# Window attention: V as the stationary operand in four column groups, fp32 probabilities streamed whole, and the bias carried through the projection

## What is computed

```python
x = x + attention(group_norm(x))        # x: 8 x 56 x 88 x 192, fp32
# group_norm: 32 groups of 6 channels, mean and variance over a whole image
# attention, on windows of 7 x 11 = 77 tokens, 8 heads of 24:
qkv  = xw @ qkv_w + qkv_b
attn = softmax(q @ k.T / sqrt(24))      # 77 x 77 for each head and window
out  = (attn @ v) merged over heads     # 77 x 192
out  = out @ proj_w + proj_b
```

## Time and profile before

| | us |
|---|---|
| median of 3 runs | 2111.34 (2107.02 to 2124.22) |
| the profiled execution, its own time | 2107.97 |
| its span, first to last instruction | 2105.9 |
| PE busy in the span | 1691.6 (80%) |
| POOL busy | 1608.9 (76%) |
| DVE busy | 1515.2 (72%) |
| ACT busy | 1299.1 (62%) |
| first and last `neg_max` of the 256 slots start at | 209.4 and 2066.0 |

### The profile page before, as it was taken

One profiled execution on the slowest core, in us unless ns is written; L12 is line 12 of the kernel. 1 busy time (PEld: TensorE's weight loads), 2 busy tenths in 40 slices (PEclk: granted clock), 3 DMA queues, 4 the chain that ended last, 5 costly groups with the idle time before them and its releaser, 6 DMA issues.

```text
span 2105.9 us, 97027 instructions
## 1 busy us (share of the span) xinstructions
PE 1691.6 (80%) x41742; PEld 1500.7 (71%) x41742; DVE 1515.2 (72%) x3672; ACT 1299.1 (62%) x2659; POOL 1608.9 (76%) x2060
## 2 busy tenths in 40 slices
PE   0003899988898888988898989988898889988886
PEld 0002788877787778877787878777787778887775
DVE  6772677777677776777777777777777777777783
ACT  0002667767676676766676766766676666767763
POOL 0004689888888898888888998988888888988864
PEclk9999899999999998999999998999999999999996
DMA  6881101111111111111111111111111111111110
GB/s 159 226 232 39 45 20 51 46 57 40 38 57 57 56 57 57 42 54 40 41 54 57 57 57 57 57 39 57 39 50 46 57 57 57 57 48 48 39 39 38
DMA packets 17134, 127.74 MB, mean 61 GB/s; under 512 B 1921, under 2 KB 2178, under 8 KB 2434
## 3 DMA queue, kind: packets, MB, share of 16 engines
q1 hardware_dynamic: 16770, 121.91, 17.1%
HBM read 91.62 MB, written 30.28 MB: 58 GB/s over the span
## 4 chain that ended last, share of the span: by engine, by line
PE 58%; DVE 26%; issue 10%; DMA 3%; ACT 1%; POOL 1%; DVEq 1%; SPq 0%; ACTq 0%; POOLq 0%
PE ps_a L676 25%; PE ps_q L676 8%; PE ps_q L775 6%; PE ps_k L676 6%; PE ps_s L715 6%; DVE v_lo L587 5%; DVE v_hi L641 5%; DVE q_lo L588 5%; DMA x_stat<-in_x 3%; PE ps_b L761 3%; DVE y_blk L627 2%; PE ps_b L676 2%; DVE q_hi L634 2%; DVE k_lo L588 2%; DVE stat L541 2%
## 5 line engine op out<-in xcount | busy, mean ns | idle before, releaser
L343 POOL TENSOR_TENSOR p_lo<-probs,p_hi 77x1232 f16<-77x1232 f32 x256 | 646.8, 2526 | 220.2 <-ACT p_hi L404 217.0
L434 ACT ACTIVATE probs<-ps_s,exp_shift,exp_scale 77x1232 f32<-77x1232 f32 x256 | 351.8, 1374 | 258.1 <-PE ps_s L715 246.1
L676 PE MATMUL ps_a<-v_hi,p_hi 77*128 77x25 f16 x4096 | 362.8, 174 | 84.6 <-DVE v_lo L587 81.9
L676 PEld LDWEIGHTS ps_a<-v_hi,p_hi 77*128 77x128 f16 x4096 | 330.1, 97 | 124.4 <-issue 122.0
L588 DVE SCALAR_TENSOR_TENSOR q_lo<-ps_q,b_qk,q_hi 128x154 f16<-128x154 f32 x512 | 170.4, 376 | 327.9 <-PE ps_q L775 327.9
L596 DVE TENSOR_REDUCE neg_max<-ps_s 77x16 fp32r<-77x1232 f32 x256 | 365.8, 1429 | 34.5 <-PE ps_s L730 34.5
L676 PE MATMUL ps_a<-v_hi,p_lo 77*128 77x25 f16 x4096 | 361.6, 174 | 0.0
L676 PE MATMUL ps_a<-v_lo,p_hi 77*128 77x25 f16 x4096 | 361.2, 174 | 0.0
L676 PEld LDWEIGHTS ps_a<-v_lo,p_hi 77*128 77x128 f16 x4096 | 323.3, 97 | 0.0
L676 PEld LDWEIGHTS ps_a<-v_hi,p_lo 77*128 77x128 f16 x4096 | 321.8, 97 | 0.0
L404 ACT ACTIVATE p_hi<-probs 77x1232 f16<-77x1232 f32 x256 | 310.0, 1211 | 0.3
(11 more groups left out here) (147 smaller groups left out, 5693.5 us busy)
## 6 DMA issues: line engine op xcount, KB each, us to landing
x_stat<-in_x SPq DMA_DIRECT2D x16, 1848.0 KB, 9.9
x_norm<-in_x SPq DMA_DIRECT2D x32, 924.0 KB
y_blk<-in_x SPq DMA_DIRECT2D x32, 924.0 KB
out<-y_blk SPq DMA_DIRECT2D x32, 924.0 KB
wA<-in_qkv_w SPq DMA_DIRECT2D x1, 288.0 KB
wB<-in_qkv_w SPq DMA_DIRECT2D x2, 144.0 KB
pA<-in_proj_w SPq DMA_DIRECT2D x1, 96.0 KB
pB<-in_proj_w SPq DMA_DIRECT2D x2, 48.0 KB
```

The lines of the kernel that those rows point to most:

```text
L343: nc.gpsimd.tensor_tensor(p_lo[(s - 1) % 2][:, 0:16 * TOK], probs[:, :], p_hi[(s - 1) % 2][:, 0:16 * TOK], ALU.subtract).then_inc(pool_p, 1)
L434: nc.scalar.activation(probs[:, :].rearrange("p (g a n) -> p g a n", g=NG, a=4), scores(), ACT.Exp, bias=exp_shift[0:TOK, :], scale=exp_sc ...
L676: last = mm(dst, lhsT, rhs, start=first and n == 0, stop=closes and n == len(pairs) - 1, skip_group_check=True)
```

## The change

The lags are set anew: attention output of i-1 instead of i-2, one slot less of buffering for it.

`attention_output` now makes V the stationary operand: `v_all`, fp32, 77 x 32 for each head and window (24 of V, one column of ones, zeros). The probabilities stream as they come from `exp`, fp32, 77 columns a matmul, with no split. The four heads g of a half write to PSUM partitions 32g to 32g+31, four column groups of the array; the output comes out transposed, channels on partitions and tokens along the free dimension. A new function `denominators` multiplies 32 columns of ones by the probabilities, 8 matmuls of 154 streamed columns, so that each of the 128 partitions gets, in `ps_b`, the denominator of each of its 308 output columns (2 heads by 2 windows by 77 tokens). DVE takes the reciprocal of all 128 x 308 of them and multiplies. The splits of P, the output's transposes, their copies, and V's split on DVE are gone (ACT copies V once). The projection uses two chunks of 128 rows with three products each, six matmuls a tile instead of five. The row of ones in the output carries the bias: `bias_hi` and `bias_lo` lie in rows 24 and 56 of the projection's weights, and POOL's bias addition is gone. The transposes of x go to `ps_k` instead of `ps_b`. The setup loads the projection weights by head group, and forms the bias's scale.

```diff
--- before.py
+++ after.py
...
-AV_LAG = 2
+AV_LAG = 1
 O_LAG = AV_LAG + 1
-T_LAG = O_LAG + 1
-P_LAG = PAIRS + O_LAG
-Y_LAG = PAIRS - 1
+P_LAG = PAIRS + O_LAG + 1
 V_BUFS = 4
 FULL = 128
 PAD = FULL - TOK
+NUM = 4 * TOK
+BIAS_ROOM = 1024.0
...
-        v_hi = [sb(f"v_hi{p}", [TOK, 2 * HEADS, HD + 1], F16) for p in range(V_BUFS)]
-        v_lo = [sb(f"v_lo{p}", [TOK, 2 * HEADS, HD + 1], F16) for p in range(V_BUFS)]
+        v_all = [sb(f"v_all{p}", [TOK, 2 * HEADS, ROW_G]) for p in range(V_BUFS)]
         neg_max = sb("neg_max", [TOK, 4, NG, ROW_G], F32R)
-        probs = sb("probs", [TOK, NG * 4 * TOK])
-        p_hi = [sb(f"p_hi{p}", [TOK, NG * 4 * TOK + PAD], F16) for p in range(2)]
-        p_lo = [sb(f"p_lo{p}", [TOK, NG * 4 * TOK + PAD], F16) for p in range(2)]
-        recip = sb("recip", [TOK, 2 * HEADS, 1])
-        o_sb = [sb(f"o_sb{p}", [TOK, 2, CH]) for p in range(2)]
-        o_split = sb("o_split", [TOK, 2, 2 * CH], F16)
+        probs = [sb(f"probs{p}", [TOK, NG, 4 * TOK]) for p in range(2)]
+        den_inv = sb("den_inv", [128, NUM])
+        o32 = [sb(f"o32_{p}", [128, NUM]) for p in range(2)]
...
-                if exists(i - 1):
-                    reach(pool, act_p, i)
-                    reach(pool, pe_av, i - 2)
-                    nc.gpsimd.tensor_tensor(p_lo[(s - 1) % 2][:, 0:16 * TOK], probs[:, :], p_hi[(s - 1) % 2][:, 0:16 * TOK],
-                                            ALU.subtract).then_inc(pool_p, 1)
                 if exists(i - O_LAG):
-                    reach(pool, act_o, i - O_LAG + 1)
-                    nc.gpsimd.tensor_tensor(o_split[:, :, CH:2 * CA], o_sb[(s - O_LAG) % 2][:, :, CA:CH], o_split[:, :, CA:CH],
-                                            ALU.subtract)
-                    nc.gpsimd.tensor_tensor(o_split[:, :, 2 * CA:3 * CA], o_sb[(s - O_LAG) % 2][:, :, 0:CA], o_split[:, :, 0:CA],
-                                            ALU.subtract).then_inc(pool_o, 1)
+                    reach(pool, act_oT, i - O_LAG + 1)
+                    o = s - O_LAG
+                    nc.gpsimd.tensor_tensor(oT_tokens(oT_lo, o), by_column(o32[o % 2]), oT_tokens(oT_hi, o),
+                                            ALU.subtract).then_inc(pool_oT, 1)
...
-                if exists(i - Y_LAG):
-                    bias = bias_out[:, :].unsqueeze(1).broadcast_to([PART, STEP_TILES[r % PAIRS][1], CH])
-                    nc.gpsimd.tensor_tensor(y, y, bias, ALU.add).then_inc(pool_y, 1)
+                    passed(dma_x[ahead % 2], base + 16 * (ahead // 2) + 16)
...
-                if exists(i - 1):
-                    reach(act, act_exp, i)
-                    reach(act, pe_av, i - 2)
-                    nc.scalar.activation(p_hi[(s - 1) % 2][:, 0:16 * TOK], probs[:, :], ACT.Copy).then_inc(act_p, 1)
-                if exists(i - T_LAG):
...
+                    last.then_inc(act_xT, 1)
                 if exists(i - O_LAG):
+                    o = s - O_LAG
                     reach(act, dve_norm, i - O_LAG + 1)
-                    nc.scalar.activation(o_split[:, :, 0:CH], o_sb[(s - O_LAG) % 2][:, :, :], ACT.Copy)\
-                        .then_inc(act_o, 1)
+                    if o % PAIRS == 0:
+                        reach(act, pe_proj, i - O_LAG - PAIRS)
+                    nc.scalar.activation(oT_tokens(oT_hi, o), by_column(o32[o % 2]), ACT.Copy).then_inc(act_oT, 1)
...
+                if exists(i):
+                    reach(act, pe_v, i + 1)
+                    nc.scalar.activation(v_all[s % V_BUFS][:, :, 0:HD],
+                                         ps_a[0:TOK, 0:2 * CH].rearrange("p (h d) -> p h d", d=HD), ACT.Copy)\
+                        .then_inc(act_v, 1)
...
                 if exists(i):
                     reach(act, pe_scoresT, i + 1)
-                    reach(act, pool_p, i)
-                    nc.scalar.activation(probs[:, :].rearrange("p (g a n) -> p g a n", g=NG, a=4), scores(),
+                    reach(act, pe_av, i - 1)
+                    nc.scalar.activation(probs[s % 2][:, :, :].rearrange("p g (a n) -> p g a n", a=4), scores(),
                                          ACT.Exp, bias=exp_shift[0:TOK, :], scale=exp_scale[0:TOK, :])\
                         .then_inc(act_exp, 1)
...
+            link(nc.vector.tensor_copy(bias_out[:, :], ps_a[:, 0:CH]))
+            link(nc.vector.tensor_reduce(bias_big[:, :], bias_out[:, :], AXIS.X, ALU.max, apply_absolute_value=True))
+            link(ts(bias_big[:, :], bias_big[:, :], 1.0 / BIAS_ROOM, None, ALU.mult))
+            link(nc.vector.reciprocal(scale_inv[:, :], big[:, 2:3]))
+            link(tt(bias_big[:, :], bias_big[:, :], scale_inv[:, :], ALU.mult))
+            link(tt(big[:, 3:4], big[:, 3:4], bias_big[:, :], ALU.max))
+            link(tt(out_scale[:, :], big[:, 2:3], big[:, 3:4], ALU.mult))
+            link(nc.vector.reciprocal(scale_inv[:, :], out_scale[:, :]))
+            link(ts(bias_out[:, :], bias_out[:, :], scale_inv[:, :], None, ALU.mult))
+            link(nc.vector.tensor_copy(bias_hi[:, :], bias_out[0:1, :]))
+            link(tt(bias_lo[:, :], bias_out[0:1, :], bias_hi[:, :], ALU.subtract))
...
+                if exists(i - O_LAG):
+                    reach(dve, pe_av, i - O_LAG + 1)
+                    reach(dve, act_oT, i - O_LAG - 1)
+                    reach(dve, pool_oT, i - O_LAG - 1)
+                    nc.vector.reciprocal(den_inv[:, :], ps_b[:, 0:NUM]).then_inc(dve_recip, 1)
+                    reach(dve, dve_recip, i - O_LAG + 1)
+                    tt(o32[(s - O_LAG) % 2][:, :], ps_a[:, 0:NUM], den_inv[:, :], ALU.mult).then_inc(dve_norm, 1)
                 if exists(i):
                     reach(dve, pe_scores, i + 1)
                     nc.vector.tensor_reduce(neg_max[:, :, :, HD:HD + 1].rearrange("p a g e -> p g (a e)"),
                                             scores(), AXIS.X, ALU.max, negate=True).then_inc(dve_max, 1)
+                if exists(i - P_LAG):
+                    r = s - P_LAG
+                    reach(dve, pe_proj, i - P_LAG + 1)
+                    if r % PAIRS == 0:
+                        reach(dve, dma_y[parity(r)], base + (r // SLOTS) * 16 + 16)
+                    y = x_step(y_blk, r)
+                    nc.vector.scalar_tensor_tensor(
+                        out=y, in0=ps_b[0:PART, 0:STEP_TILES[r % PAIRS][1] * CH].rearrange("p (c d) -> p c d", d=CH),
+                        scalar=out_scale[0:PART, :], in1=y, op0=ALU.mult, op1=ALU.add).then_inc(dve_out, 1)
                 if exists(i):
...
-                if exists(i - AV_LAG):
-                    reach(dve, pe_av, i - AV_LAG + 1)
-                    reach(dve, pool_o, i - AV_LAG - 1)
-                    av = ps_a[0:TOK, 0:2 * HEADS * (HD + 1)].rearrange("p (h e) -> p h e", e=HD + 1)
-                    nc.vector.reciprocal(recip[:, :, :], av[:, :, HD:HD + 1]).then_inc(dve_recip, 1)
-                    reach(dve, dve_recip, i - AV_LAG + 1)
-                    tt(o_sb[(s - AV_LAG) % 2][:, :, :].rearrange("p w (h d) -> p (w h) d", d=HD), av[:, :, 0:HD],
-                       recip[:, :, :].broadcast_to([TOK, 2 * HEADS, HD]), ALU.mult).then_inc(dve_norm, 1)
...
-                v_now, p_now = s % V_BUFS, s % 2
                 for j in range(NJ):
                     for g in range(NG):
-                        h, at = HEADS * w + NG * j + g, (4 * g + 2 * w + j) * TOK
-                        last = products(ps_a[:, h * (HD + 1):(h + 1) * (HD + 1)], (
-                            (p_hi[p_now][:, at:at + FULL], v_hi[v_now][:, h, :]),
-                            (p_hi[p_now][:, at:at + FULL], v_lo[v_now][:, h, :]),
-                            (p_lo[p_now][:, at:at + FULL], v_hi[v_now][:, h, :])))
+                        at = (2 * w + j) * TOK
+                        o = ps_a[ROW_G * g:ROW_G * (g + 1), 2 * j * TOK:2 * (j + 1) * TOK]\
+                            .rearrange("p (c w r) -> p c w r", c=WIN_W, w=2)[:, :, w, :]
+                        last = mm(o, v_all[s % V_BUFS][:, HEADS * w + NG * j + g, :], probs[s % 2][:, g, at:at + TOK],
+                                  start=True, stop=True, skip_group_check=True)
+                return last
+            def denominators(s):
+                for w in range(2):
+                    for g in range(NG):
+                        d = ps_b[ROW_G * g:ROW_G * (g + 1), 0:NUM].rearrange("p (a w r) -> p a w r", w=2, r=WIN_H)
+                        last = mm(d[:, :, w, :], ones[0:TOK, 0:ROW_G], probs[s % 2][:, g, 2 * w * TOK:2 * (w + 1) * TOK],
+                                  start=True, stop=True, skip_group_check=True)
                 return last
...
+                if exists(i - P_LAG):
+                    if exists(i - O_LAG):
+                        reach(pe, dve_recip, i - O_LAG + 1)
+                    else:
+                        reach(pe, dve_out, i - P_LAG)
+                    r = s - P_LAG
+                    if r % PAIRS == 0:
```

(60 more changed lines are left out.)

177 lines of the change are left out of this document (60 added, 117 removed).

## The result

| | before | after |
|---|---|---|
| median of 3 runs, us | 2111.34 | 2734.18 (2728.89 to 2736.08) |
| span of the profiled execution, us | 2105.9 | 2732.6 |
| mean granted TensorE clock | 0.937 | 0.841 |
| starts of the first and the last `neg_max`, us | 209.4 and 2066.0 | 218.4 and 2691.3 |

The change makes the kernel slower: the ratio of the times is 1.2927, with a 95% interval of 1.2835 to 1.3019. The prediction was 2605 us, between 2380 and 2900.

What follows compares the result with a forecast made beforehand. PE and DVE, each waiting for the other in turn, were taken to bound the kernel, neither alone. From 2108 us, 320 for the longer loop, 172 for clock falls and 5 for setup and end gave 2605 us, range 2380 to 2900.

Steps and rivals of the forecast that it cites:

- hand-over, way through the array and projection: Behind the reciprocal: 0.07 + 0.17 us until PE's first projection matmul is through, then 0.50 us of projection a tile.
- window 1 with the denominators: PE's fp32 column-group matmuls on the loop's path: window 1 of the attention output 0.30 us, denominators 0.55 us, together 0.85 us.
- the 20 to 25% that I named as a sign: Sign that the forecast is right: DVE's reciprocal holds near 20 to 25% of the chain by line.
- The rival on that side: DVE's division costs no more than another pass over PSUM, 0.46 us; the kernel gets faster, 2021 us; chance 0.04.
- the 0.82 us from which the sign turns: Length of DVE's reciprocal below which the change would make the kernel faster, given no more clock falls.
- The lower end of my bounds: For window 1 and denominators on PE: 0.77 us if a round's four groups run beside one another; upper bound 2.9 us.
- the rival in which groups take turns: PE's column groups do not overlap: window 1 and denominators cost at least 3.1 us, total 3180 us; chance 0.12.
- Two drains at my estimated 0.17 us: Possible waits on PE's path where the tiling mode changes into and out of column groups; would add 90 us.
- 172 us more for the falls: PE's clock falls in every second slot because PE stands still for the reciprocal; 1.34 us a fall, 172 us.
- My reason for the middle: Every second slot taken: PE's idle time is longer than in any undisturbed slot before, but shorter than 3.2 us.
- the clock falls in each slot or more: A slower slot has more idle parts, so PE's clock falls again: 2777 us, up to some 2900 us; chance 0.12.

Runs made afterwards that it cites:

- experiment 4: The changed kernel with 24 f16 matmuls, whose result nobody reads, added between the scores and the output projection: 2391.17 us, ratio 1.1322.
- experiment 1: The changed kernel with its reciprocal replaced by a multiplication with a constant on the same tile, so the division is left out: 2031.86 us, ratio 0.9623.
- experiment 8: The changed kernel with a constant multiplication for the reciprocal, and all four heads of a half written to one column group: 2680.50 us, ratio 1.2709.
- experiment 7: The changed kernel with the fp32 matmuls reordered, so that the two of one column group stand next to each other: 2770.95 us, ratio 1.3138.
- experiment 2: The changed kernel with the reciprocal taken of 154 of the 308 columns, the other half holding a constant: 2211.96 us, ratio 1.0476.

## Why the prediction was right

**The loop.** The terms come back as they were summed: reciprocal 2.07 us taken, 2.083 measured; hand-over, way through the array and projection 0.74 taken, 0.04 + 0.70 measured; V 0.91 and 0.82; K 0.68 and 0.68; row maxima 0.48 and 0.43; `q_lo` with its hand-over 0.74 and 0.72; transposed scores 0.53 and 0.60; Q 0.79 and 0.79; window 1 with the denominators 0.85 and 0.98. The sum, 7.85 us, measured as 7.92. With two tiles the undisturbed slot is 8.41 us (experiment 4), so the mean over the mix is 8.10 us, where I had 8.04. Before, slots of one and of two tiles both took 6.79 us: the slot in the earlier trace rows has two tiles, as its `y_blk` of 112 x 384 shows, and the one around this row has one, between `neg_max` at 1204.63 and 1211.42.

```profile
1209.18 0.40 DVE L627 SCALAR_TENSOR_TENSOR y_blk<-ps_b,out_scale,y_blk 112x192 f32<-112x192 f32 x1
```

So the loop costs (8.10 - 6.79) x 255 = 335 us, where I had 320.

**The reciprocal.** Its price could be worked out from two rows of a different size, and experiment 1 shows that it alone sets the sign. Its share of the chain is 18% of the span, a little under the 20 to 25% that I named as a sign, since the span is longer than forecast. The rival on that side was worked out as 2021 us, and a kernel with the cheap division took 2031.86. It did not happen, since 2.08 us is over the 0.82 us from which the sign turns. By the repeat count of the Trainium skill (VectorE: DVE Perf Modes, "First, the fixed hardware budget") it would have been an estimated 2.57 us; the measured price is 6.2 ns a column where that count gives an estimated 8.3, and 2.083 us in all.

**The column groups.** The lower end of my bounds was the right one (0.98 us within 0.77 to 2.9), and the rival in which groups take turns is refuted by experiment 8, not by experiment 7. The drain at a change of tiling mode (the Trainium skill, TensorEngine Tiling (Array Packing), "Key Properties") does not show as a gap: the pieces of row groups, whole array, column groups and again column groups start at 1215.41, 1216.01, 1216.80 and 1217.21, each where the one before ended. Two drains at my estimated 0.17 us would be 0.34 us, and the column pieces came only 0.13 us over my price. No run tells whether a shorter drain lies inside them.

**The clock: the term that was off.** I took 172 us more for the falls than the kernel before had, every second slot at 1.34 us. What lies above the undisturbed loop is (9.70 - 8.10) x 255 = 407 us in the changed kernel, and (7.28 - 6.79) x 255 = 125 us before; the 281 us between them are what that term should have been. Away from the turns of the hardware loop it is 294 us against 53, and in experiment 4 it is 2 us, so there the fill takes away all of it. Two things were too small. Four slots in five are disturbed. And a fall costs 1.62 us and not 1.34, because the slow work is V, K and the row maxima, which all stand on the path. My reason for the middle, that the idle time is shorter than the 3.2 us of the earlier trace rows, was no reason: a wait for a reciprocal of 2.08 us in every slot is enough here, and for one of 1.12 us mostly it is not (experiment 2).

Of the 129 us between forecast and result, 109 are the clock's, 15 the loop's and 5 the setup's (10 us measured, with the end, where I had 5). The loop and the reciprocal were worked out; that the result lies inside the range is owed to the upper case, the rival "the clock falls in each slot or more" (2777 us). It came nearest, and I had given it 0.12.

## What to carry to other kernels

When a change makes the busiest engine wait for another in every turn of a loop, look at what it does to the granted clock as well as at the length of the wait: here the longer turn of the loop cost 335 us and the slow work behind the wait most of a further 281 us, and moving work that was there anyway into the wait gave back 365 us. Price a reciprocal by its columns, from whichever reciprocals the trace has, before it takes the place of several cheap instructions. And when two remedies are put together, follow the queue of the engine that each of them leans on: each came out well alone, and together they were 165 us worse than the better one.
